# Cross attention on one core: masks as four 64x64 products with shifted heads, and the maxima's score units as two products of 64 rows each

## The chip, the core and the metric

The kernel is one program on one core of a Trainium2 chip. Its engines run beside one another and meet only through semaphores: TensorE (PE in the rows; its weight loads are PEld), VectorE (DVE), ScalarE (ACT), GpSimd (POOL) and SyncE (SP). The metric is the device time of one execution, in microseconds (us), as a median over runs. The change touches the first of two phases, the cross attention.

## The reference

For each of 16 batch rows, 256 tokens of 128 numbers attend to 1600 keys and one more, in 16 heads of 8 dimensions each; a gated residual follows, and then six layers of a second network, which the change leaves alone.

```python
# x (16,256,128), ctx (16,1601,128), mask (16,1,256,1601), NEG = -1e9
def _L0_xattn_ref(q, k, v, mask, ...):
    qh = _split_heads(q @ w_q + b_q)
    kh = _split_heads(k @ w_k + b_k)
    vh = _split_heads(v @ w_v + b_v)
    scores = einsum('bhqd,bhkd->bhqk', qh, kh) / sqrt(8)
    scores = where(mask, NEG, scores)
    attn = softmax(scores, axis=-1)
    out = einsum('bhqk,bhkd->bhqd', attn, vh)
    ...
    return out @ w_o + b_o
x = x + tanh(g_xattn[0]) * _L0_xattn_ref(_layernorm(x), ctx, ctx, mask, ...)
x = x + tanh(g_ffn[0]) * _L0_ffn_ref(_layernorm(x), ...)      # six layers
```

## The kernel before

**Rows, groups and steps.** `cross_phase` works through the 16 batch rows as a pipeline. An `iteration` has a current row `cur`, whose exponentials and products run, a next row `nxt`, which is prepared, and a previous one `prev`, which is finished. It has four parts q = 0 to 3 (four heads each) of KT = 13 steps kt = 0 to 12 (128 keys each, the last 65), 52 steps in all. A step is written (q, kt) here.

**Exact scores in bf16.** Queries and keys are split into three bf16 parts. All nine products of parts are stacked along the contraction, so a head's scores are one product of 9 x 8 = 72 rows; the operands are `q_op` and `k_op`.

**What PE does in a step, in this order.**
1. *Score units* (L736). To find each query's maximum, scores are computed once with queries on the partitions: per four heads 16 units (two tiles of 128 queries, four heads, two halves of the keys), spread over 13 steps by `units_of`. A unit fills one of the two buffers `b_s` with 1024 or 577 columns; DVE adds the mask `mq` and takes the maximum (L509). They run ahead: from step (2, 7) on (TURN = 7) the units are those of `nxt`'s first four heads, and the wait for their operands stands there (`at == 0`).
2. *Transposed scores*, in two halves i = 0, 1 of two heads each and a bank `b_e[i]` of their own: the mask as an identity times `mk`, 512 columns (L750), then two score products of 75 rows and 256 columns (L754; three rows carry minus the maximum). ACT takes the exponential of each half (L436). A mask product waits until ACT has read the same bank in the step before.
3. *Value products* of the step before (L656): four of 9 columns, in four column tiles of the array side by side (an fp32 product is issued as two matmuls).
4. In 20 of the 52 steps one use of the bank `b_p` (`uses`): four for the maxima's transposition, four for keys (L681), four for values (L688), three for the query and its norm, five for the previous row.

**The orders of SP and ACT.** SP's list in an iteration is written out. Keys go to `k_scr` in DRAM and return as `k_op[q]`, one buffer for each q, by three DMAs of 24 rows (L264); queries go to `q_scr` and return as `q_op` by nine DMAs of 8 rows (L319), issued once the last exponential inputs of q = 1 are done. ACT issues three small DMAs with the maxima in each q after step 9 (L480), in its own order, so exponentials stand behind them.

## Time and profile before

| | us |
|---|---|
| median of 3 runs | 5792.77 (5790.32 to 5793.39) |
| the profiled execution | 5784.99 |
| its span in the profile | 5783.2 |
| PE busy in the span | 5490.1 (95%) |
| ACT, DVE, POOL busy | 3995.5, 3631.9, 2653.2 |

The cross attention takes the first 1990 us or so of the span (about 14 of the page's 40 slices). PE is busy in nearly all of it; a busy PE is not PE at its peak, since the ends of pipelined matmuls are modelled. So in the timeline the distance from one start to the next is what a group costs, not its length.

### The profile page before, as it was taken

The page shows a single profiled execution, that of the slowest core. Times are in us where ns is not written, and L with a number is a line of the kernel's source. Part 1 is how long each engine was busy: PE and PEld are TensorE (multiplying, and loading weights), DVE is VectorE, ACT ScalarE, POOL GpSimd, SP SyncE. Part 2 cuts the span into 40 slices and gives each one's busy share as a digit, 9 for nine tenths or more (in the row PEclk, how much of TensorE's full clock was granted, in tenths as well). Part 3 has the DMA queues.
Part 4 walks back from the last instruction along what each step waited for, and adds up shares of the span by engine and source line. Part 5 has one row for each costly group of instructions (what it writes and reads, how often), then busy time and mean ns, then how long its engine had stood idle before and what let it go on. Part 6 is the DMA issues. An engine that isn't in the chain of part 4 may idle for free.

```text
span 5783.2 us, 146589 instructions
## 1 busy us (share of the span) xinstructions
PE 5490.1 (95%) x51848; PEld 3278.6 (57%) x51848; DVE 3631.9 (63%) x8009; ACT 3995.5 (69%) x10790; POOL 2653.2 (46%) x2284
## 2 busy tenths in 40 slices
PE   5999999999999789999999999999999999999997
PEld 2444444444444356666666666666666666666665
DVE  3666776677667456666666666666666666656664
ACT  2555555555555478787887778787888788878885
POOL 2211221112211166656665666666666666665663
PEclk9999999999999899999999999999999999999999
DMA  3232222222332133333333333333333333333332
GB/s 85 61 71 74 57 73 67 74 64 66 74 75 63 54 103 97 100 104 108 97 100 99 108 100 101 94 109 103 102 93 108 104 104 93 97 115 103 93 98 89
DMA packets 144825, 517.35 MB, mean 89 GB/s; under 512 B 29884, under 2 KB 46140, under 8 KB 125676
## 3 DMA queue, kind: packets, MB, share of 16 engines
q1 hardware_dynamic: 142572, 507.58, 31.0%
q8 instruction: 427, 7.00, 0.5%
q14 instruction: 290, 2.38, 0.1%
q10 hardware_dynamic: 1536, 0.40, 0.0%
HBM read 224.98 MB, written 30.68 MB: 44 GB/s over the span
## 4 chain that ended last, share of the span: by engine, by line
PE 44%; ACT 12%; issue 6%; DVE 2%; POOL 1%; DMA 0%; SPq 0%; ACTq 0%; DVEq 0%; POOLq 0%
PE b_qk L1442 9%; PE b_c L1483 6%; PE b_pt L1381 5%; PE b_o L1401 5%; ACT probs L1144 5%; PE b_sc L1369 4%; PE b_nv L1417 3%; PE b_qk L1453 3%; PE b_sc L1360 2%; ACT L1183 2%; ACT L79 2%; PE b_c L1513 2%; PE b_nv L1513 1%; ACT ln_n L1109 1%; PE b_c L1488 1%
## 5 line engine op out<-in xcount | busy, mean ns | idle before, releaser
L436 ACT ACTIVATE eT<-b_e 128x512 f32<-128x512 f32 (+1 forms) x1664 | 903.2, 594 | 871.5 <-PE b_e L754 751.2
L1144 ACT ACTIVATE probs<-b_sc,nb,rq 128x96 f32<-128x96 f32 (+1 forms) x3072 | 1322.5, 449 | 8.7 <-DVE nb L1277 7.5
L509 DVE CUSTOM_DVE_ANT_0 junk<-b_s,mq 128x1024 bf16<-128x1024 f32 (+1 forms) x1024 | 998.9, 990 | 373.3 <-PE b_s L736 359.1
L1068 POOL TENSOR_TENSOR probs<-probs,rsums 128x512 f32<-128x512 f32 (+1 forms) x768 | 717.2, 934 | 666.4 <-DVE rsums L1213 665.9
L1268 DVE TENSOR_REDUCE b_sc<-b_sc 128x4 f32<-128x512 f32 (+1 forms) x768 | 486.1, 633 | 837.6 <-PE b_sc L1369 837.5
L1131 ACT ACTIVATE probsT<-b_pt 128x512 f32<-128x512 f32 x768 | 455.9, 594 | 579.7 <-PE b_pt L1381 579.7
L1442 PE MATMUL b_qk<-xs,weights 128*128 128x256 f32 x3072 | 740.3, 384 | 59.5 <-ACT sq L1158 31.8
L750 PE MATMUL b_e<-mk,identb 128*128 128x512 bf16 (+1 forms) x1664 | 636.7, 383 | 20.6 <-ACT eT L436 19.9
L1144 ACT ACTIVATION_READ_ACCUMULATOR probs<-b_sc,nb,rq 128x1 f32 x3072 | 645.9, 210 | 0.0
L754 PE MATMUL b_e<-q_op,k_op 75*128 75x256 bf16 (+1 forms) x3328 | 639.8, 273 | 0.0
L1442 PEld LDWEIGHTS b_qk<-xs,weights 128*128 128x128 f32 x3072 | 556.4, 191 | 144.9 <-issue 74.5
L1401 PEld LDWEIGHTS b_o<-probsT,v 128*64 128x64 f32 x9216 | 373.0, 137 | 453.3 <-issue 453.3
L1247 DVE TENSOR_TENSOR rot_s<-b_qk,rot_tab 128x512 f32<-128x512 f32 x768 | 525.3, 684 | 127.2 <-PE b_qk L1442 114.7
L1037 POOL TENSOR_TENSOR kT<-kT,rot_p 128x1024 f32<-128x1024 f32 x192 | 454.6, 2368 | 306.1 <-DMA rot_p<-rot_s 302.5
L1401 PE MATMUL b_o<-probsT,v 128*64 128x64 f32 (+1 forms) x9216 | 515.7, 247 | 34.2 <-DVE oT L1205 26.9
L736 PE MATMUL b_s<-k_op,q_op 72*128 72x512 bf16 (+1 forms) x2048 | 504.0, 343 | 27.2 <-DVE smax L509 13.7
L1158 ACT ACTIVATE sq<-b_qk 128x512 f32<-128x512 f32 x768 | 439.1, 599 | 125.1 <-DVE kT L1253 65.5
L656 PE MATMUL b_pv<-eT,vx 128*9 128x256 f32 x6656 | 518.1, 383 | 2.8 <-ACT eT L436 2.8
L1381 PE MATMUL b_pt<-ident,probs 128*128 128x128 f32 x3072 | 504.0, 287 | 1.1 <-POOL probs L1068 1.1
L1045 POOL TENSOR_TENSOR kT<-kT,rkb 128x1024 f32<-128x1024 f32 x192 | 452.1, 2355 | 110.8 <-DMA rkb<-rk_scr 110.8
L1037 POOL TENSOR_TENSOR qT<-qT,rot_p 128x1024 f32<-128x1024 f32 x192 | 453.0, 2359 | 89.5 <-DMA rot_p<-rot_s 70.4
L754 PEld LDWEIGHTS b_e<-q_op,k_op 75*128 75x128 bf16 (+1 forms) x3328 | 332.4, 100 | 252.5 <-issue 5.2
(133 smaller groups left out, 8348.8 us busy)
## 6 DMA issues: line engine op xcount, KB each, us to landing
rot_p<-rot_s SPq DMA_DIRECT2D x768, 256.0 KB, 2.4
rkb<-rk_scr SPq DMA_DIRECT2D x192, 512.0 KB, 6.4
k_op<-k_scr SPq DMA_DIRECT2D x192, 300.2 KB
v<-v SPq DMA_DIRECT2D x192, 256.0 KB, 3.6
k_scr<-kp SPq DMA_DIRECT2D x48, 400.2 KB, 3.5
weights<-in_ffn_w SPq DMA_DIRECT2D x27, 512.0 KB, 5.0
ctxT<-in_ctx SPq DMA_DIRECT2D x17, 800.5 KB, 8.7
q_op<-q_scr SPq DMA_DIRECT2D x144, 64.0 KB
```

The costliest lines, as they stand in the source:

```text
L436: nc.scalar.activation(eT[0:n, g % 2, i * 512:(i + 1) * 512], b_e[i][0:n, :], ACT.Exp).then_inc(s["e_ready"], 1)
L509: nc.vector.tensor_tensor_reduce(junk[:, half, 0:n], b_s[u % 2][:, 0:n], mq[:, p, qt, half * 1024:half * 1024 + n], 1.0, LOWEST, ALU.add, ...
L656: last = nc.tensor.matmul(b_pv[32 * h:32 * h + DK + 1, 0:S], vx[0:n, p, kt, 4 * q + h, :], eT[0:n, g % 2, h * S:(h + 1) * S], start=(kt == ...
L750: nc.tensor.matmul(b_e[i][0:n, :], identb[0:n, 0:n], mk[0:n, p, kt, :].unsqueeze(1).to_broadcast([n, 2, S]), start=True, stop=False, skip_ ...
L754: last = nc.tensor.matmul(b_e[i][0:n, j * S:(j + 1) * S], k_op[q][0:MROW + 3, 2 * i + j, kt * P:kt * P + n], q_op[0:MROW + 3, p, 4 * q + 2 ...
L1037: nc.gpsimd.tensor_tensor(dst, dst, rot_p[:, i % 2, :].rearrange("p (j t) -> p j t", j=4), ALU.add).then_inc(s["sum_ready"], 1)
L1068: nc.gpsimd.tensor_tensor(pu, pu, rsums[:, u % 2, :].unsqueeze(2).to_broadcast([P, 4, w]), ALU.mult).then_inc(s["pn_ready"], 1)
L1144: last = nc.scalar.activation(probs[:, t, k % 2, 2 * e + h, c0:P], b_sc[:, 512 * e + h * w:512 * e + (h + 1) * w], ACT.Exp, bias=nb[:, k % ...
L1247: nc.vector.tensor_tensor(per_block(rot_s[:, q % 2, 512 * (i % 2):512 * (i % 2 + 1)]), per_block(src), rot_tab[:, tab + 1, :].unsqueeze(1) ...
L1381: last = nc.tensor.transpose(b_pt[:, i * P:(i + 1) * P], probs[:, t, u % 2, i, :], ident[:, :])
L1401: last = nc.tensor.matmul(b_o[r, o0 + q0:o0 + q1], v[:, p, tile, vc], probsT[:, u % 2, c + q0:c + q1], start=True, stop=True, skip_group_c ...
L1442: last = nc.tensor.matmul(b_qk[:, 512 * (i % 2) + x * S:512 * (i % 2) + (x + 1) * S], weights[:, c0:c0 + P], xs[:, p, :], start=True, stop ...
```

## The change

- **Masks as quarters (L793 after).** A full mask tile is now four products of 64 rows and 64 columns of the array, 512 columns long: for b_e[0] the two on the diagonal, for b_e[1] the two off it. Off the diagonal, keys come out shifted by 64, so the two heads of i = 1 work on keys kt x 128 + 64 on. `k_op`, `ctxT` and `mk` are longer by 64 keys (wrapped around), and the values of every second pair of heads are computed for shifted keys: each value product of 128 columns becomes two of 64. All four mask quarters stand ahead of both halves' scores.
- **Score units (L770 after).** A unit is two products of 64 rows and 401 columns, one from rows 0 to 63 and one from rows 64 to 127, into two banks. The smallest of the nine products of parts is left out, which gives 64 rows. The operands are new: `k_s`, two buffers with the key's two halves on the two halves of the partitions, and `q_s`, which holds the queries twice. DVE reads 2 x 401 columns for every unit.
- **Loads.** `k_op` has two buffers in place of four. For each q, ten DMAs load `k_s` beside the three for `k_op`; for each row, 16 DMAs of 8 rows load `q_s` beside the nine for `q_op`. SP's list is written anew around these.

PE's order in one step with one unit. Before (the names: b_s the units' banks, b_e the transposed scores, b_pv the values):

```order
L736 MATMUL b_s<-k_op,q_op 128x512 [waits s_max]
L736 MATMUL b_s<-k_op,q_op 128x512
L736 MATMUL b_s<-k_op,q_op 128x512 [waits s_max]
L736 MATMUL b_s<-k_op,q_op 128x65
L750 MATMUL b_e<-mk,identb 128x512 [waits e_ready]
L754 MATMUL b_e<-q_op,k_op 128x256 x2
L750 MATMUL b_e<-mk,identb 128x512 [waits e_ready]
L754 MATMUL b_e<-q_op,k_op 128x256 x2
L656 MATMUL b_pv<-eT,vx 9x256 [waits e_ready]
L656 MATMUL b_pv<-eT,vx 9x256 x3
```

That step has two units. One of the changed kernel, with one unit:

```order
L770 MATMUL b_s<-k_s,q_s 128x401 [waits s_max]
L770 MATMUL b_s<-k_s,q_s 128x401
L793 MATMUL b_e<-mk,identb 64x512 [waits e_ready]
L793 MATMUL b_e<-mk,identb 64x512
L793 MATMUL b_e<-mk,identb 64x512 [waits e_ready]
L793 MATMUL b_e<-mk,identb 64x512
L805 MATMUL b_e<-q_op,k_op 128x256 x4
L688 MATMUL b_pv<-eT,vx 9x256 [waits e_ready]
L688 MATMUL b_pv<-eT,vx 9x256 x3
```

The mask of the second half, with its wait for ACT, now stands ahead of the first half's scores.

SP's list from the start of q = 2 (e_done) to the end of q = 2. Before:

```order
L310 DMA q_scr<-qp 128x256 x2
L319 DMA q_op<-q_scr 8x4096 [waits start_in,e_done,qscr_in]
L319 DMA q_op<-q_scr 8x4096 x8
L264 DMA k_op<-k_scr 24x6404 x3
L264 DMA k_op<-k_scr 24x6404 [waits e_done,start_in]
L264 DMA k_op<-k_scr 24x6404 x2
```

After:

```order
L343 DMA q_scr<-qp 128x256 x2
L280 DMA k_s<-k_scr 16x4x801 [waits e_done,s_done,kscr_in]
L280 DMA k_s<-k_scr 16x4x801 x2
L283 DMA k_s<-k_scr 8x4x801 x2
L280 DMA k_s<-k_scr 16x4x801 x3
L283 DMA k_s<-k_scr 8x4x801 x2
L286 DMA q_s<-q_scr 8x4096 [waits qscr_in]
L286 DMA q_s<-q_scr 8x4096 x15
L272 DMA k_op<-k_scr 24x6660 x3
L263 DMA ctxT<-in_ctx 128x1665 [waits vx_ready]
```

Where nine DMAs of `q_op` stood, ten of `k_s` and 16 of `q_s` stand now; `q_op` moved to the start of q = 3, where `k_s` and `k_op` of the next row stand ahead of it.

```diff
--- before.py
+++ after.py
+TURNED = DH
+KEXT = KEYS + TURNED
+CHUNK = 401
+S_HALF = 800
+S_KEYS = S_HALF + 1
+MASKED = 4 * CHUNK
...
-        k_op = [sb(f"k_op{i}", [P, 4, KEYS], BF16) for i in range(4)]
+        k_op = [sb(f"k_op{i}", [P, 4, KEXT], BF16) for i in range(2)]
+        k_s = [sb(f"k_s{i}", [P, 4, S_KEYS], BF16) for i in range(2)]
+        q_s = sb("q_s", [P, 2, HX, S], BF16)
...
             def load_k(b, p, q):
                 src = k_scr[p].rearrange("c (d h) k -> (c d) h k", d=DK)[:, 4 * q:4 * q + 4, :]
                 for a in range(3):
-                    sp.dma_start(k_op[q][24 * a:24 * a + 24, :, :], src).then_inc(kop_in[q], 16)
-
-
+                    sp.dma_start(k_op[q % 2][24 * a:24 * a + 24, :, :], src).then_inc(kop_in[q % 2], 16)
+
+            def load_ks(b, p, q):
+                src = k_scr[p].rearrange("c (d h) k -> (c d) h k", d=DK)[:, 4 * q:4 * q + 4, :]
+                for tile in range(2):
+                    keys = slice(S_HALF * tile, S_HALF * tile + S_KEYS)
+                    for a in range(3):
+                        r = DH * tile + 16 * a
+                        sp.dma_start(k_s[q % 2][r:r + 16, :, :], src[0:16, :, keys]).then_inc(ks_in[q % 2], 16)
+                    for a in range(2):
+                        r = DH * tile + 48 + 8 * a
+                        sp.dma_start(k_s[q % 2][r:r + DK, :, :], src[16:24, :, keys]).then_inc(ks_in[q % 2], 16)
+
+            def load_q_parts(dst, r, p, a, done):
+                sp.dma_start(dst[r:r + DK, p, :, :], q_scr[p, a].rearrange("(d h) q -> d h q", d=DK)
+                             ).then_inc(s[done], 16)
+
+            def load_qs(p):
+                for tile in range(2):
+                    for a in range(3):
+                        for c in range(2):
+                            load_q_parts(q_s, DH * tile + 16 * a + DK * c, p, a, "qs_in")
+                    for a in range(2):
+                        load_q_parts(q_s, DH * tile + 48 + DK * a, p, a, "qs_in")
...
+            def load_q(p):
+                for a in range(3):
+                    for c in range(3):
+                        load_q_parts(q_op, 24 * a + DK * c, p, a, "qop_in")
...
+                if cur:
+                    sp.wait_ge(s["s_done"], count("s_done", cur[0], 48))
+                    sp.wait_ge(s["e_done"], count("e_done", cur[0], 4 * KT))
                 if nxt:
                     b, p = nxt
-                    sp.wait_ge(start_in, 48)
-                    sp.wait_ge(s["e_done"], count("e_done", b, 6 * KT, back=1))
-                    load_k(b, p, 2)
-                    sp.wait_ge(start_in, 48)
+                    load_ks(b, p, 0)
+                    sp.wait_ge(s["qscr_in"], count("qscr_in", b, 48))
+                    load_qs(p)
+                if cur:
+                    load_k(*cur, 3)
+                if nxt:
+                    b, p = nxt
                     sp.wait_ge(s["vx_ready"], count("vx_ready", b, 4))
                     load_ctx(b + 1)
-                    sp.wait_ge(start_in, 48)
+                    if cur:
+                        sp.wait_ge(s["s_done"], count("s_done", cur[0], 64))
+                        sp.wait_ge(s["e_done"], count("e_done", cur[0], 6 * KT))
+                    load_ks(b, p, 1)
+                    load_k(b, p, 0)
+                    load_q(p)
...
                         nc.vector.tensor_tensor_reduce(
-                            junk[:, half, 0:n], b_s[u % 2][:, 0:n], mq[:, p, qt, half * 1024:half * 1024 + n],
+                            junk[:, half, :].rearrange("p (c n) -> p c n", c=2),
+                            b_s[u % 2][:, :].rearrange("p (c n) -> p c n", c=2)[:, :, 0:CHUNK],
+                            mq[:, p, qt, 2 * CHUNK * half:2 * CHUNK * half + 2 * CHUNK].rearrange("p (c n) -> p c n", c=2),
                             1.0, LOWEST, ALU.add, ALU.max, smax[:, half, 4 * qt + h:4 * qt + h + 1]
...
-                            last = nc.tensor.matmul(b_p[0:n, t * P:(t + 1) * P], ctxT[:, k0:k0 + n],
-                                                    w_sb[:, XW_V:XW_V + P], start=True, stop=True)
+                            wv = w_sb[:, XW_V:XW_V + P].rearrange("p (g i e) -> p g i e", g=4, i=2)
+                            to = b_p[0:n, t * P:(t + 1) * P].rearrange("p (g i e) -> p g i e", g=4, i=2)
+                            for i2 in range(2):
+                                last = nc.tensor.matmul(to[:, :, i2, :], ctxT[:, k0 + TURNED * i2:k0 + TURNED * i2 + n],
+                                                        wv[:, :, i2, :], start=True, stop=True)
...
-                                pe.wait_ge(kop_in[sq], b * KOP + KOP)
-                                pe.wait_ge(s["qop_in"], count("qop_in", b, 9 * 16))
+                                pe.wait_ge(ks_in[sq % 2], (2 * b + sq // 2 + 1) * KS)
+                                pe.wait_ge(s["qs_in"], count("qs_in", b, 16 * 16))
                             for u in units_of(at):
                                 qt, h, half = u // 8, (u // 2) % 4, u % 2
 
                                 pe.wait_ge(s["s_max"], count("s_max", b, 16 * sq + u - 1))
                                 for c in range(2):
-                                    k0 = half * 1024 + c * 512
-                                    n = min(512, KEYS - k0)
-                                    last = nc.tensor.matmul(b_s[u % 2][:, c * 512:c * 512 + n],
-                                                            q_op[0:MROW, p, 4 * sq + h, qt * P:(qt + 1) * P],
-                                                            k_op[sq][0:MROW, h, k0:k0 + n], start=True, stop=True)
+                                    r = slice(c * DH, (c + 1) * DH)
+                                    last = nc.tensor.matmul(b_s[u % 2][:, 512 * c:512 * c + CHUNK],
+                                                            q_s[r, p, 4 * sq + h, qt * P:(qt + 1) * P],
+                                                            k_s[sq % 2][r, h, 400 * half:400 * half + CHUNK],
+                                                            start=True, stop=True)
                                 last.then_inc(s["s_done"], 1)
                         if cur:
                             b, p = cur
                             n = tile_keys(kt)
                             g = q * KT + kt
                             if kt == 0:
+                                pe.wait_ge(kop_in[q % 2], (2 * b + q // 2 + 1) * KOP)
+                                pe.wait_ge(s["qop_in"], count("qop_in", b, 9 * 16))
                                 pe.wait_ge(s["mk_ready"], count("mk_ready", b, 1))
                                 pe.wait_ge(s["mrow_in"], count("mrow_in", b, 48 * (q + 1)))
+                            if n == P:
+
+                                pe.wait_ge(s["e_ready"], count("e_ready", b, 2 * g - 1))
+                                for i in range(2):
+                                    if i:
+                                        pe.wait_ge(s["e_ready"], count("e_ready", b, 2 * g))
+                                    for to in range(2):
+                                        frm = (to + i) % 2
+                                        r, ro = slice(frm * DH, (frm + 1) * DH), slice(to * DH, (to + 1) * DH)
+                                        nc.tensor.matmul(b_e[i][ro, :], identb[r, r],
+                                                         mk[r, p, kt + (i and to), :].unsqueeze(1).to_broadcast([DH, 2, S]),
+                                                         start=True, stop=False, skip_group_check=True)
                             for i in range(2):
 
-                                pe.wait_ge(s["e_ready"], count("e_ready", b, 2 * g + i - 1))
-                                nc.tensor.matmul(b_e[i][0:n, :], identb[0:n, 0:n],
-                                                 mk[0:n, p, kt, :].unsqueeze(1).to_broadcast([n, 2, S]),
-                                                 start=True, stop=False, skip_group_check=True)
+                                if n < P:
+                                    pe.wait_ge(s["e_ready"], count("e_ready", b, 2 * g + i - 1))
+                                    nc.tensor.matmul(b_e[i][0:n, :], identb[0:n, 0:n],
+                                                     mk[0:n, p, kt + i, :].unsqueeze(1).to_broadcast([n, 2, S]),
+                                                     start=True, stop=False, skip_group_check=True)
+                                k0 = kt * P + TURNED * i
                                 for j in range(2):
                                     last = nc.tensor.matmul(
-                                        b_e[i][0:n, j * S:(j + 1) * S], k_op[q][0:MROW + 3, 2 * i + j, kt * P:kt * P + n],
+                                        b_e[i][0:n, j * S:(j + 1) * S], k_op[q % 2][0:MROW + 3, 2 * i + j, k0:k0 + n],
```

## Rows read from the trace of the kernel before

**Rows 1.** Busy time in one stretch (columns in its first line).
```profile
core 0: us, PE busy (x) PEld busy (x) DVE busy (x) ACT busy (x) POOL busy (x), PEclk, DMA share, GB/s
880.00:1000.00 120.00, 118.21 (x939) 53.20 (x938) 83.99 (x165) 64.56 (x119) 23.68 (x26) 1.00 0.29 70
```

**Rows 2.** Timeline, PE and ACT, part of a step: start, length us, what, count.
```profile
1002.37 0.38 PE L754 MATMUL b_e<-q_op,k_op 75*128 75x256 bf16 x2
...
1002.59 0.38 PE L750 MATMUL b_e<-mk,identb 128*128 128x512 bf16 x1
...
1002.79 1.08 ACT L436 ACTIVATE eT<-b_e 128x512 f32<-128x512 f32 x2 [1.14 <-PE b_e L754]
1002.81 0.38 PE L754 MATMUL b_e<-q_op,k_op 75*128 75x256 bf16 x2
...
1003.12 0.62 PE L656 MATMUL b_pv<-eT,vx 128*9 128x256 f32 x8
...
1003.67 0.60 PE L736 MATMUL b_s<-k_op,q_op 72*128 72x512 bf16 x2
```

**Rows 3.** Timeline, PE, the first step of q = 2.
```profile
989.08 0.38 PE L754 MATMUL b_e<-q_op,k_op 75*65 75x256 bf16 x2
...
989.94 0.42 PE L736 MATMUL b_s<-k_op,q_op 72*128 72x512 bf16 x2
```

**Rows 4.** Timeline, SP issuing DMAs, in this row and in the next.
```profile
989.55 2.99 SPq L319 DMA_DIRECT2D q_op<-q_scr  x9
992.58 1.12 SPq L264 DMA_DIRECT2D k_op<-k_scr  x3
...
1107.14 2.99 SPq L319 DMA_DIRECT2D q_op<-q_scr  x9
```

**Rows 5.** Busy time around two batches of loads (columns of Rows 1).
```profile
989.40:990.40 1.00, 1.00 (x12) 0.35 (x12) 0.64 (x2) 0.73 (x2) 0.00 (x0) 1.00 0.00 0
990.40:993.40 3.00, 3.00 (x30) 1.34 (x28) 2.04 (x4) 1.68 (x4) 0.00 (x0) 1.00 0.57 98
990.40:1004.90 14.50, 14.50 (x122) 6.29 (x120) 9.52 (x21) 7.74 (x15) 0.00 (x0) 1.00 0.65 105
977.60:983.60 6.00, 6.00 (x55) 3.01 (x53) 3.64 (x7) 3.26 (x6) 3.22 (x6) 1.00 0.79 178
```

**Rows 6.** Timeline, PE, four 64x64 products in the later phase.
```profile
3002.28 0.30 PE L1360 MATMUL b_sc<-lmask,identb 64*64 64x256 bf16 x4
```

**Rows 7.** DVE instructions by shape: busy us, mean ns | idle before.
```profile
L509 DVE CUSTOM_DVE_ANT_0 junk<-b_s,mq 128x1024 bf16<-128x1024 f32 x512 | 626.1, 1223 | 272.6 <-PE b_s L736 260.9 <-DVE smax L588 8.3 <-issue 3.0
```

**Rows 8.** Timeline, PE, one v unit and what follows.
```profile
1086.46 1.16 PE L688 MATMUL b_p<-w_sb,ctxT 128*128 128x128 f32 x8
1087.45 0.60 PE L736 MATMUL b_s<-k_op,q_op 72*128 72x512 bf16 x2
```

**Rows 9.** Timeline, ACT, steps 9 and 10 of q = 2.
```profile
1008.71 1.09 ACT L436 ACTIVATE eT<-b_e 128x512 f32<-128x512 f32 x2 [0.89 <-PE b_e L754]
1009.68 1.80 ACTq L480 DMA_DIRECT2D q_op<-mp  x3
1011.58 1.09 ACT L436 ACTIVATE eT<-b_e 128x512 f32<-128x512 f32 x2 [1.78 <-PE b_pv L656]
```

**Rows 10.** Timeline, PE, the start of the first row.
```profile
62.20 1.50 PE L736 MATMUL b_s<-k_op,q_op 72*128 72x512 bf16 x4 [12.33 <-issue]
```

**Rows 11.** Timeline, ACT and PE, end of an idle stretch, first row.
```profile
125.53 1.08 ACT L436 ACTIVATE eT<-b_e 128x512 f32<-128x512 f32 x2 [5.73 <-issue]
...
126.18 0.39 PE L750 MATMUL b_e<-mk,identb 128*128 128x512 bf16 x1 [3.42 <-ACT eT L436]
```

**Rows 12.** Timeline, PE, after an idle stretch at the phase's end.
```profile
1984.26 3.66 PE L717 MATMUL b_p<-ru,w_sb 128*128 128x256 f32 x8 [8.81 <-DVE ru L603]
```

**Rows 13.** Granted clock after these two (columns of Rows 1).
```profile
127.40:141.00 13.60, 13.60 (x61) 5.03 (x54) 4.52 (x10) 5.91 (x11) 5.89 (x2) 0.50 0.47 145
1984.30:1987.60 3.30, 3.30 (x8) 2.45 (x8) 0.00 (x0) 0.00 (x0) 0.00 (x0) 0.50 0.00 0
```

More of the change, by code:

```diff
@@ L70 @@
 X_NVEC = 4
-N_SETX = 2
+N_SETX = 1
+N_SETD = 3
 EXP_LN_TABLES = 6
@@ L268, in _ @@
+            def load_q(p):
+                for a in range(3):
+                    for c in range(3):
+                        load_q_parts(q_op, 24 * a + DK * c, p, a, "qop_in")
             load_ctx(0)
             load_masks(0)
-            sp.wait_ge(set_pool, N_SETX)
-            for i in range(4):
-                sp.dma_start(k_op[i][MROW:MROW + 3, :, :], onesr[:, :].unsqueeze(1).to_broadcast([3, 4, KEYS])
-                             ).then_inc(ones_in, 16)
+            sp.wait_ge(set_dve, N_SETD)
@@ L504, in s_units @@
                         qt, h, half = u // 8, (u // 2) % 4, u % 2
-                        n = 1024 if half == 0 else KEYS - 1024
                         dve.wait_ge(s["s_done"], count("s_done", b, 16 * sq + u + 1))
```

99 lines of the change are left out of this document (49 added, 50 removed).

## The prediction

> **What bounds the kernel now.** I read the timeline of PE first, then who waits for whom, then SP's list of DMAs with the stretches around it. In the cross attention PE is busy for 118.2 of 120 us at full clock, DVE for 84, ACT for 64.6, and the DMA engines move 70 GB/s [rows 1]. So PE sets the pace, and what takes work off PE is worth its full length until something else is late. A batch row repeats every 117.6 us: the nine DMAs of `q_op` are issued at 989.55 and again at 1107.14 [rows 4].
>
> In the timeline of a step the reader is to see distances from start to start. Mask to scores 0.22 us, two score products 0.22, the second pair 0.31 up to the value products, and these 0.55 up to the next unit [rows 2]. The second pair takes 0.09 more than the first, though it is the same work: behind it PE goes from full columns to column tiles. Two pairs of scores (0.53), two masks (0.44) and the values (0.55) are 1.52 us. From the first unit of (2, 0) at 989.94 to that of (2, 7) at 1003.67 there are 7 steps in 13.73 us, 1.96 each [rows 2, 3]; so score units cost 0.44 a step.
>
> **What the change takes off PE.** A unit has 800 columns on average before; two products of 401 side by side take half, so 0.44 becomes 0.22. The masks: in the later phase four 64x64 products of 256 columns last 0.30 us together, from the first start to the last end, less than the 0.38 of one full mask of 512 [rows 2, 6]. So quarters do run side by side, and four of 512 columns should cost about one mask, 0.22 in place of 0.44.
>
> Against that stand two more changes of tiling in a step (units to quarters, quarters to full scores), 0.09 each by the step from scores to values: 0.18. PE's own step is then 0.22 + 0.22 + 0.18 + 0.53 + 0.55 = 1.70 us. If such a change cost nothing it would be 1.52, and I know no reason for more than the 0.09 seen.
>
> **What is late next.** All mask quarters now stand ahead of the first half's scores, so these wait until ACT has read both banks of the step before. The loop: first score pair to ACT's start 0.42 (1002.37 to 1002.79), two exponentials 1.08, ACT's end to PE's mask 0.06 (half of the pair's 1.08 after 125.53 is 126.07, the mask starts at 126.18, so 0.11 at most; I take 0.06, since the two overlap a little), masks 0.22, tiling 0.09: 1.87 us [rows 2, 11]. That is more than 1.70. A plain step falls from 1.96 to 1.87 only, and half of the freed time turns into a wait for ACT. In the 20 steps that also use `b_p` PE has more to do (and one more change of tiling, 0.09) and stays the bound: 1.79 in place of 1.96.
>
> DVE reads 802 columns per unit, at 1223 ns for 1024 [rows 7] about 0.96 us where the mean was near that already; its 84 us in 120 cover it. POOL's masks grow by a few per cent and have slack (23.7 of 120 busy [rows 1]). I cost both at nothing.
>
> Per batch row:
> - 25 plain steps outside the stretch (2, 0) to (2, 6): 25 x -0.09 = -2.3 us.
> - 20 steps with `b_p`: 20 x -0.17 = -3.4 us.
> - Values: 26 more matmuls of 64 columns with 128-column loads. A unit of eight now takes 0.99 us to the next start, 0.12 each [rows 8]. If the weight load sets that pace, they cost 26 x 0.12 = +3.1; if the moving columns do, 0. I take 3.1: 128 columns of fp32 have to be loaded as before.
> - The maxima's DMAs: ACT issues three in 1.80 us after step 9, and the next exponentials start 1.78 us after the last ended, where 0.89 is usual [rows 9]. PE does not show that now. In a loop that hangs on ACT it does: 1.78 - (1.87 - 1.08) = 1.0 us. Twice in full (q = 2, 3), twice half covered by `b_p` work in step 9 (q = 0, 1): 3.0, less 0.6 that I allow for what is lost already: +2.4. Bounds 0 and 4.
>
> **The stall.** The first unit of the next row, at (2, 7), needs `q_s` and `k_s`. SP may start them only when q = 1's scores are done, and in the trace it issues 0.47 us after the last pair (989.08 to 989.55); no byte moves before 990.4, 0.85 us on [rows 3 to 5]. Before, nine `q_op` DMAs (9 x 64 = 576 KB) had to be there by 1003.67. Now it is ten of `k_s` (128 rows of 4 x 801 bf16, 820 KB) and then 16 of `q_s` (1024 KB), on one queue.
> - `q_op` alone moved at 98 GB/s, with `k_op` behind it at 105; `k_op` alone in 977.6 to 983.6 (some small writes beside it) at 178 [rows 5]. `q_s` has exactly the shape of `q_op` (8 rows of 8 KB): 1024 KB / 98 = 10.4 us. `k_s`, short pieces of 1.6 KB, lies between 178 and 98: 4.6 to 8.4 us. I take the mixed 105, 7.8 us.
> - Landed at 990.4 + 18.2 = 1008.6, where the unit started at 1003.67: +4.9 us. Bounds: 15.0 us of transfer give +1.7, 18.8 give +5.5.
> PE takes its instructions in order, so behind this wait stand all scores and values; ACT and DVE drain, and nothing covers it. The seven steps before it become faster, but that only lengthens the wait.
>
> The DMA engines' busy share was 0.57 while `q_op` ran alone, against 0.79 for `k_op` [rows 5]: DMAs of 8 rows leave many engines idle. The Trainium skill, "DMA: Bandwidth & Descriptors", section "Why a DMA increments its semaphore by 16 and not by 1", says that a DMA runs on the largest number of engines up to 16 that divides its outer sizes, the lowest-numbered ones; so 8 rows go to the same 8 engines each time, and the trace agrees. If that did not hold and `q_s` ran at 178 GB/s, all would have landed at 1000.8, ahead of need.
>
> **Clock.** After 3.42 us without PE work the granted clock was 0.50 (1.2 in place of 2.4 GHz) for the 13.6 us of 127.4 to 141.0, with PE busy in all of it; after an idle 8.81 us it was still 0.50 for 3.3 us of work [rows 11 to 13]. At half clock half the work is lost: 6.8 and 1.7 us. The stall is between these in length; I take 3.0 a row, bounds 0 and 6.8.
>
> **Sum.** -2.3 - 3.4 + 3.1 + 2.4 + 4.9 + 3.0 = +7.7 us a row, in 15 iterations that have a next row: +115. The very first units start after 12.33 us without PE work, at 62.20 [rows 10]; they now wait for `k_s` (7.8 us) and seven more DMAs of 64 KB (4.6), +12; the last row, with no stall and fewer units, gives back about 6. Together +121 us on the profiled execution's 5785, so 5906. The median of the runs shown is 7.8 us above that execution: 5914 us, 2.1% slower.
>
> **The rivals.**
> 1. *The loads arrive in time.* For it: the batch 977.6 to 983.6 ran at 178 GB/s. Against: DMAs of just this shape did not. At that rate landing is 1000.8, no stall, no lost clock; in the stretch (2, 0) to (2, 6) the steps gain 7 x 0.09 = 0.6. -2.3 - 3.4 - 0.6 + 3.1 + 2.4 = -0.8 a row, -12: 5781. With values and ACT's DMAs free as well, -6.3 a row: 5698. Other side of the forecast; it decides from 18.2 us of transfer down to about 12.5. Chance 0.24.
> 2. *The quarters, or a unit's two products, do not overlap.* Both quarters of a bank come from different rows of the array at once. In the later phase the rows write different banks, so the trace does not show this case. If they take turns, the masks cost 0.44 again, PE's step is 1.91: 25 plain steps lose 0.04 each and 20 others 0.22, +5.4 a row, +81: 5995. The Trainium skill, "TensorEngine Tiling (Array Packing)", "Restrictions and Gotchas", says that different row tiles cannot use the same PSUM bank simultaneously; by it this rival would be the case. Here the two write different partitions of the bank, which is why I give it less. Chance 0.14.
> 3. *The stall is there, but short and at full clock,* and values follow the moving columns: -2.3 - 3.4 + 0 + 2.4 + 1.7 = -1.6 a row, with +6 for the start: 5775. Chance 0.06.
> The forecast itself has 0.56; with its costs at their far ends (clock 6.8, stall 5.5) it reaches 5980. Its own range is 5850 to 5980.
>
> A difference under 0.2% (12 us) can't be told from none. Of rival 1, about half lies within that (5781 is at its edge), half is faster; rival 3 is faster; the forecast's low edge gives a little to "same". Faster 0.20, same 0.10, slower 0.70. The range for 8 in 10: 5755 to 5995.
>
> **What would show it.** In the profile after: at each (2, 7) PE idle for about 5 us ahead of the unit, released by the `q_s` DMAs, with the clock at 0.50 behind it; plain steps of 1.87 us with waits of the masks for ACT; the four quarters within about 0.4 us of each other's ends; 0.09 us at each change of tiling; 16 value matmuls at 0.11 to 0.12 us. The forecast is wrong if `q_s` lands before step (2, 7), if the clock holds through the stall, or if PE's steps come near 1.70 us.

## The result, and the profile after

The changed kernel takes 6128.8 us (median of 4 runs, 6102.7 to 6200.5) against 5792.4 us before: a ratio of 1.0566, 95% interval 1.0519 to 1.0613, 336 us more. The forecast was 5914 us with a range up to 5995. The execution that was profiled is the slowest of the four, 6200.5 us, more than 1.5% above the fastest, so the ratio leaves it out; e6 and e7 below show what is said of the clock in runs near their medians. Against the 5785 us of the profiled one before it takes 415 us more, and the sums below are made against these; 72 us of them lie above the median.

I read the stall first. PE at step (2, 7) of one row (columns as in [rows 2]):

```profile
start us, us, engine line op out<-in xcount [idle before <-releaser]
1042.89 0.62 PE L688 MATMUL b_pv<-eT,vx 128*9 128x256 f32 x8
1054.27 0.52 PE L770 MATMUL b_s<-k_s,q_s 64*128 64x401 bf16 x2 [10.75 <-DMA q_s<-q_scr]
1054.71 0.64 PE L793 MATMUL b_e<-mk,identb 64*64 64x512 bf16 x4
```

It is where the forecast put it and is released by `q_s`, but lasts 10.75 us and not 4.9. The length of a step is counted here from its first exponential to that of the next step, so a wait ahead of one step lengthens the one before: this stall shows in step (2, 6). Over rows 1 to 14 that step takes 12.18 us on average where it took 1.97 before: 10.2 us more. SP's issues ahead of it:

```profile
1029.93 1.27 SPq L280 DMA_DIRECT2D k_s<-k_scr  x3
...
1033.95 5.38 SPq L286 DMA_DIRECT2D q_s<-q_scr  x16
1039.37 1.12 SPq L272 DMA_DIRECT2D k_op<-k_scr  x3
1040.54 0.36 SPq L263 DMA_DIRECT2D ctxT<-in_ctx  x1
```

In the list of packets `k_s` moves from 1030.9 to 1037.7 and `q_s` from 1037.2 to 1052.9. The stretches (the seventh number is the granted clock, then DMA share and GB/s):

```profile
core 0: us, PE busy (x) PEld busy (x) DVE busy (x) ACT busy (x) POOL busy (x), PEclk, DMA share, GB/s
1030.80:1037.10 6.30, 6.30 (x64) 2.46 (x60) 5.03 (x10) 3.28 (x7) 0.00 (x0) 1.00 0.78 128
1037.10:1053.00 15.90, 6.41 (x66) 2.27 (x64) 4.39 (x11) 4.32 (x8) 0.00 (x0) 0.84 0.86 117
1054.30:1081.90 27.60, 27.60 (x166) 7.67 (x166) 11.68 (x24) 9.56 (x18) 2.48 (x5) 0.50 0.35 72
1082.10:1105.60 23.50, 20.41 (x198) 7.50 (x194) 13.84 (x29) 10.95 (x21) 2.50 (x5) 1.00 0.82 127
```

The third row is the larger surprise: behind the stall PE is busy for 27.6 us without a gap, and the clock stays at 0.50 (1.2 GHz) all that time. [Rows 13] showed 13.6 us at most. Two more waits were on no list of mine: ahead of the masks of (0, 0), here of the next row, and of (0, 11), which is inside the step counted as (0, 10):

```profile
1105.67 0.48 PE L793 MATMUL b_e<-mk,identb 64*64 64x512 bf16 x4 [2.61 <-DMA q_op<-mp]
...
991.42 0.89 PE L793 MATMUL b_e<-mk,identb 64*64 64x512 bf16 x4 [1.41 <-ACT eT L466]
```

The first waits for the three small DMAs of the maxima, which ACT issued 10 us earlier, at 1095.61. The second was there before, a little shorter and with the clock full behind it, as PE's timeline of the kernel before has it:

```profile
1073.33 0.39 PE L750 MATMUL b_e<-mk,identb 128*128 128x512 bf16 x1 [0.97 <-ACT eT L436]
```

Now the clock falls behind it too. A steady step of the changed kernel, PE's timeline, and ACT's in a like step:

```profile
1084.22 0.60 PE L793 MATMUL b_e<-mk,identb 64*64 64x512 bf16 x4
1084.76 0.61 PE L805 MATMUL b_e<-q_op,k_op 75*128 75x256 bf16 x4
1085.30 0.62 PE L688 MATMUL b_pv<-eT,vx 128*9 128x256 f32 x8
1085.85 0.34 PE L770 MATMUL b_s<-k_s,q_s 64*128 64x401 bf16 x2
1086.12 0.60 PE L793 MATMUL b_e<-mk,identb 64*64 64x512 bf16 x4
...
1094.82 1.08 ACT L466 ACTIVATE eT<-b_e 128x512 f32<-128x512 f32 x2 [0.82 <-PE b_e L805]
```

1.90 us from mask to mask, of which ACT works 1.08 and waits 0.82 for the scores: the loop of the forecast. Where nothing waits, quarters to scores take 0.34 us (1082.51 to 1082.85); here 0.54, the rest being a wait for ACT.

The account of a row, from the first exponentials of one row to those of the next (mean of rows 1 to 14): 117.7 us before, 144.7 after, +27.0. The steps' medians at full clock, stall left out, add up to 119.2, which is +1.6; the stall is +10.2; what is left, **+15.2, is the half clock** and the waits at (0, 0). Fourteen times 27.0 is 379 us; row 0 adds 13, the start 8, the last row 7 and the phase behind it 8, together the 415. PE was busy at half clock for 574 us of the cross attention, before for 17 us.

### The profile page after: what moved, and what is told of

Read it like the earlier page. It is cut to its first block, busy times and chain, and to the rows that moved or that the text cites. A ratio compares the mean times of both kernels' runs of the same rounds, so it can differ in the third digit from the quotient of the medians.

```text
span 6198.7 us, 151308 instructions
## 1 busy us (share of the span) xinstructions
PE 5710.0 (92%) x53800; PEld 3254.5 (53%) x53800; DVE 3640.5 (59%) x8011; ACT 4004.0 (65%) x10790; POOL 2661.7 (43%) x2283
## 4 chain that ended last, share of the span: by engine, by line
PE 41%; ACT 12%; issue 5%; DVE 2%; POOL 1%; DMA 0%; SPq 0%; ACTq 0%; DVEq 0%; POOLq 0%
PE b_qk L1493 9%; PE b_c L1534 6%; PE b_pt L1432 5%; PE b_o L1452 5%; ACT probs L1195 4%; PE b_sc L1420 3%; PE b_nv L1468 3%; PE b_qk L1504 3%; PE b_sc L1411 2%; ACT L1234 2%; ACT L86 2%; PE b_c L1564 2%; PE b_nv L1564 1%; ACT ln_n L1160 1%; PE b_c L1539 1%
## 5 line engine op out<-in xcount | busy, mean ns | idle before, releaser
L540 DVE CUSTOM_DVE_ANT_0 junk<-b_s,mq 128x802 bf16<-128x802 f32 x1024 | 998.4, 991 | 571.1 <-PE b_s L770 558.0
L805 PE MATMUL b_e<-q_op,k_op 75*128 75x256 bf16 (+1 forms) x3328 | 588.0, 302 | 0.0
L688 PE MATMUL b_pv<-eT,vx 128*9 128x256 f32 x6656 | 578.9, 424 | 2.8 <-ACT eT L466 2.7
L770 PE MATMUL b_s<-k_s,q_s 64*128 64x401 bf16 x2048 | 355.2, 375 | 173.5 <-DMA q_s<-q_scr 147.4
L387 POOL CAST mp<-mneg 4x256 bf16<-4x256 f32 x64 | 27.7, 432 | 1106.0 <-DVE mneg L555 1106.0
L793 PE MATMUL b_e<-mk,identb 64*64 64x512 bf16 x3072 | 421.0, 442 | 65.9 <-DMA q_op<-mp 30.7
```

The costliest lines, as they stand in the source:

```text
L540: nc.vector.tensor_tensor_reduce(junk[:, half, :].rearrange("p (c n) -> p c n", c=2), b_s[u % 2][:, :].rearrange("p (c n) -> p c n", c=2)[ ...
L688: last = nc.tensor.matmul(b_pv[32 * h:32 * h + DK + 1, 0:S], vx[0:n, p, kt, 4 * q + h, :], eT[0:n, g % 2, h * S:(h + 1) * S], start=(kt == ...
L805: last = nc.tensor.matmul(b_e[i][0:n, j * S:(j + 1) * S], k_op[q % 2][0:MROW + 3, 2 * i + j, k0:k0 + n], q_op[0:MROW + 3, p, 4 * q + 2 * i ...
```

## The experiments

"Half clock" is the time in the cross attention in which PE was busy at the granted clock 0.50, summed from the trace; the changed kernel has 574 us (676 with its idle time, the figure that some expectations name). A "gap" is an idle time of PE. Each ratio is to runs of the kernel before that were taken beside the run.

| run | kernel | us (median) | ratio, 95% interval | half clock, us |
|---|---|---|---|---|
| e1 | changed, loads early | 5966.2 | 1.030 (1.024-1.036) | 291 |
| e2 | e1 with whole masks | 5821.9 | 1.006 (1.004-1.007) | 65 |
| e3 | before, with quarters | 6008.2 | 1.034 (1.028-1.040) | 347 |
| e4 | before, with a stall | 6078.4 | 1.050 (1.049-1.052) | 104 |
| e5 | changed, whole masks | 5987.7 | 1.034 (1.032-1.035) | 158 |
| e6 | changed, values undoubled and unshifted | 6063.5 | 1.044 (1.039-1.049) | 413 |
| e7 | changed, q_s by 16 rows, read twice | 6255.8 | 1.078 (1.072-1.084) | 449 |
| e8 | e2, such loads, spread | 5953.2 | 1.027 (1.026-1.029) | 106 |
| e9 | e5, values doubled, masks ahead of scores | 6037.0 | 1.043 (1.041-1.044) | 165 |
| e10 | changed, copies of q | 6054.3 | 1.046 (1.045-1.048) | 369 |
| e11 | e2, copies, spread | 5878.9 | 1.015 (1.014-1.017) | 121 |
| e12 | e2, spread | 5845.0 | 1.009 (1.008-1.011) | 104 |
| e13 | e1, copies, gated, list reordered | 5874.8 | 1.014 (1.011-1.017) | 188 |
| e14 | e2, copies, gated, list reordered | 5742.6 | 0.992 (0.991-0.994) | 9 |
| e15 | e2, gated, list reordered | 5765.7 | 0.996 (0.994-0.997) | 45 |

**e1: the loads early.** Only the place of one wait differs:

```diff
                     sp.wait_ge(s["s_done"], count("s_done", cur[0], 48))
-                    sp.wait_ge(s["e_done"], count("e_done", cur[0], 4 * KT))
 ...
                 if cur:
+                    sp.wait_ge(s["e_done"], count("e_done", cur[0], 4 * KT))
                     load_k(*cur, 3)
```

> The changed kernel with one difference: SP no longer waits for q = 1's scores (e_done 4 KT) ahead of k_s and q_s of the next row, but only ahead of k_op for q = 3, which now follows them. The loads can start at step (1, 6) in place of (2, 0), 25 us ahead of the units that need them, for 18 to 21 us of data. Theory 1 (the loss is the loads' stall at (2, 7), about 10 us a row, and the half clock that it and the smaller waits bring): no gap of PE at (2, 7), steps at full clock as they were (their medians in the changed kernel add up to 119.2 us a row, stall left out), so 5785 + 15 x 1.6 + 10 for the start = about 5820 us (5780 to 5870), half-clock time in the cross attention under 150 us. Rival A (the sparser steady state of quarters and half units drops the clock by itself): the stall goes, 10 us a row, but the clock still falls for 300 us or more: 5950 to 6050 us. Rival B (the stall is not the price, the steps are): about 6100 us.

Measured 5966 us, with 291 us of half clock. The stall at (2, 7) is gone from every row (step (2, 6) 1.90 us), but this gave back 163 us and no more. So theory 1 alone is out; the time is rival A's, but the run does not show that the stream loses the clock by itself, as small waits are left. New ones stand at (2, 0), 2 to 5 us in nine of 14 rows, and at (0, 0), 1 to 3.3 us, for the maxima's DMAs:

```profile
1134.71 0.59 PE L793 MATMUL b_e<-mk,identb 64*64 64x512 bf16 x4 [3.20 <-DMA q_op<-mp]
```

**e2 and e3: one half of the change each.** In e2 the masks and values are as before:

```diff
-                                        nc.tensor.matmul(b_e[i][ro, :], identb[r, r], ...   # four quarters
+                                nc.tensor.matmul(b_e[i][0:n, :], identb[0:n, 0:n],
+                                                 mk[0:n, p, kt, :].unsqueeze(1).to_broadcast([n, 2, S]), ...
```

> Only the score units of the change (two products of 64 rows from k_s and q_s), masks as one 128x128 product each and values undoubled as in the kernel before; loads early as in e1_early. PE's step by the terms of the forecast: 1.96 - 0.22 + 0.09 = 1.83 us, above ACT's loop since each mask waits for its own bank alone. Theory 1: no stall, full clock, 52 steps a row at -0.13 in the 40 that PE bounds = -5 us a row, 15 rows: 5792 - 78 + 10 for the start = 5725 us (5690 to 5770). Rival A (row tiles of 64 rows by themselves cost clock): half clock in more than a tenth of the cross attention, 5850 us or more. Rival B: the change of tiling eats the gain, 5785 to 5810 us.

Measured 5822: outside all three ranges, between rivals B and A, with little half clock, but a wait of up to 5.5 us ahead of the masks of (0, 0), the step (3, 12), released by `q_op<-mp` (48 us of idle in all). e3 has the quarters, the shifted heads and the doubled values in the kernel before, with its own units and loads:

> Only the masks of the change (64x64 quarters with shifted heads, doubled value products), score units and all loads as in the kernel before. Nothing is loaded in addition, so no stall at (2, 7). Theory 1: full clock; plain steps 1.90 to 1.92 us in place of 1.96, three value steps at +0.7 each: between -0.5 and +1.5 us a row, 5785 to 5815 us. Rival A (a PE that waits a little for ACT in each step loses the clock): half clock for 100 us or more in the cross attention, 5880 us or more.

Measured 6008: rival A in size (5880 or more), but not in form. Ten rows run at full clock, 122.6 us each: +5.0 on the row before. Two rows take 195 and 190 us (below one row at full clock, then a part of the second slow one):

```profile
1640.00:1760.00 120.00, 118.13 (x1020) 49.31 (x1016) 81.12 (x159) 62.51 (x114) 22.88 (x24) 1.00 0.28 69
1800.80:1960.00 159.20, 159.19 (x826) 53.11 (x827) 57.49 (x121) 48.37 (x90) 17.95 (x20) 0.50 0.19 47
```

In the second stretch PE is never idle, and the clock does not return for 160 us. It had fallen behind a gap of 1.3 us. So quarters and doubled values by themselves cost 5 us a row at full clock, and a half clock that has begun can last longer than a row with PE busy all the time.

**e4: a stall in the dense kernel.** 22 DMAs of `q_op`'s shape to a place that nobody reads:

```diff
+                    for c in range(SPARE):            # 22
+                        r = DK * (c % 16)
+                        sp.dma_start(spare[r:r + DK, c // 16, :, :], q_scr[p, 0].rearrange(...)).then_inc(spare_in, 16)
                     for a in range(3):                # q_op
```

> The kernel before, with 22 DMAs of 8 rows (64 KB each, read by nobody) issued ahead of the nine of q_op in each row. At q_op's measured 98 GB/s they take 14.7 us, so q_op lands at about 1011 where the unit started at 1003.7: a stall of 7.3 us at (2, 7) in PE's otherwise full stream. Theory 1: the stall also halves the clock for about 10 to 20 us a row behind it; 15 x (7.3 + 5 to 10) + 15 for the start = +200 to +275: 5990 to 6070 us. Rival A (the clock is lost only by the sparser stream of the changed kernel): the stall alone, 15 x 7.3 + 15 = +125, 5917 us, half clock under 3 us a row. If the extra DMAs run faster than q_op's did, there is no stall and 5792.

The gaps are twice what I worked out, 15.3 us in the median:

```profile
1162.12 1.01 PE L745 MATMUL b_s<-k_op,q_op 72*128 72x512 bf16 x2 [16.73 <-DMA q_op<-q_scr]
```

but behind them the half clock lasts only 4.8 us (3.7 to 6.7), where the changed kernel has 13.1 (3.4 to 28.0) behind gaps of 10.3. The total of 6078, 8 us above theory 1's range, is mostly gap (15 x 15.3 = 230 of 288 us). It comes near theory 1's number for the wrong reason, and rival A's 5917 is out too.

**e5, e6, e9: the same stall in front of other streams.** Whole masks (e5), undoubled values (e6, which leaves out the values' shift and so computes other values), whole masks with doubled values (e9), each in the changed kernel with its late loads.

> The changed kernel with its loads as late as they were, but each mask one 128x128 product again and the values undoubled: the same stall of about 10 us at each (2, 7), in front of another stream. Theory 1 (a stall costs its half clock whatever follows): half clock of about 45 us a row as in the changed kernel (676 us in all), 5950 to 6030 us. Theory 2, new after e3 and e4 (the stall or small wait only starts the half clock; how long it lasts depends on what PE then runs, and the 64x64 quarters keep it): half clock of 5 to 10 us a row behind each stall as in e4, under 200 us in all: 5822 of e2 + 15 x (10 + 3) = 5960 to 6020 us with under 200 us of half clock. The half-clock time and its length per event decide, not the total.

> The changed kernel with 13 value products of 128 columns as before, in place of 26 of 64: this leaves out the shift of the values by 64 keys for every second head. It takes away the term of +3.1 us a row (measured +2.1 by the steps (1, 3), (1, 5), (1, 9)). If that is all: 15 x -2 = -30 us on 6129, about 6095 us, and half clock as long as before. If the small weight-bound products are what prolongs the half clock rather than the mask quarters: half clock less than half of 676 us and 5950 us or less.

> The changed kernel, stall, doubled values and order kept, with each step's four mask quarters replaced by two products of 128x128 (both still ahead of the scores); the shift by 64 keys is left out of the second mask. If the quarters are what keeps the half clock: behind each stall of 10 us about 5 us of busy half clock as in e5 (13 in the changed kernel), none after waits of 1 to 1.5 us, half clock under 300 us in all, 5990 to 6050 us. If it is the doubled values or the longer wait for ACT: half clock above 450 us, 6080 to 6150 us.

| | gap at (2, 7), median | half clock behind it, median (range) |
|---|---|---|
| changed | 10.3 us | 13.1 us (3.4-28.0) |
| e6, quarters | 7.9 | 13.1 (3.4-15.2) |
| e7, quarters (below) | 16.8 | 11.7 (4.5-26.8) |
| e5, whole masks | 10.3 | 4.9 (3.5-6.5) |
| e9, whole masks | 10.5 | 5.0 (3.4-6.5) |

One stretch of e5 and one of e9, right behind a gap of 11.23 and of 10.5 us:

```profile
1107.53 0.52 PE L767 MATMUL b_s<-k_s,q_s 64*128 64x401 bf16 x2 [11.23 <-issue]
...
1107.60:1111.00 3.40, 3.40 (x18) 0.98 (x17) 1.00 (x2) 1.19 (x2) 0.00 (x0) 0.50 0.57 123
1111.20:1150.00 38.80, 34.75 (x309) 13.34 (x308) 24.52 (x51) 19.52 (x36) 4.96 (x10) 0.98 0.69 115
```

```profile
999.70:1003.30 3.60, 3.60 (x18) 0.96 (x17) 1.00 (x2) 1.09 (x2) 0.00 (x0) 0.50 0.60 130
1003.60:1030.00 26.40, 25.94 (x232) 10.31 (x230) 18.04 (x38) 14.62 (x28) 3.36 (x7) 1.00 0.62 112
```

e9 differs from the changed kernel in the quarters alone (the second mask's shift, which it leaves out, changes values and not work), and the long half clock is gone: theory 2 holds. e6 keeps the quarters and keeps most of it, 413 us. Its 65 us of gain are more than the 30 expected, but its gap is shorter by 2.4 us in the mean too, and with the 2.1 us of the value steps that is 15 x 4.5 = 67 us. Whether the doubled values also add to the half clock is not settled.

**e7 and e8: q_s by DMAs of 16 rows.**

```diff
-                        for c in range(2):
-                            load_q_parts(q_s, DH * tile + 16 * a + DK * c, p, a, "qs_in")
+                        sp.dma_start(q_s[r:r + 16, p, :, :], q_scr[p, a].rearrange("(d h) q -> d h q", d=DK)
+                                     .unsqueeze(0).to_broadcast([2, DK, HX, S])).then_inc(s["qs_in"], 16)
```

> The changed kernel with q_s loaded by 8 DMAs of 16 rows in place of 16 of 8 rows: the same bytes, source rows read twice by one DMA, nothing moved. The forecast took 10.4 us for q_s because DMAs of 8 rows use half of the engines. If that was right, q_s lands in 5 to 6 us less, the gap at (2, 7) falls from about 10 to about 5 us, but the half clock behind it mostly stays: 15 x -5 = -75 us, 6020 to 6080 us. If the number of rows is not what limits q_s (Rival), the gap stays 9 to 11 us and the time 6100 to 6160 us.

> e2 with the loads spread: q_s by 8 DMAs of 16 rows and q_op by 3 of 24 rows, q_op ahead of the next k_s, so that the maxima's small DMAs no longer stand behind a backlog at (3, 9). In e2 the last step lasts 4.6 us where it lasted 2.58, and (0, 1) runs at half clock in 11 of 14 rows. Theory: that wait goes (2.0 us a row) and the 72 us of half clock with it (2.4 a row): 5822 - 15 x 4.4 = 5756 us (5735 to 5785), faster than the kernel before. Rival (the small DMAs are late for another reason): 5810 to 5825 us.

Both missed (6020 to 6080 and 5735 to 5785 were expected), by my own making. e7's gap grew to 16.8 us in the median, 17.20 in this row, and `q_s` took 23 us, at a DMA share of 0.49:

```profile
1077.00:1100.00 23.00, 6.38 (x66) 2.27 (x64) 4.35 (x11) 4.28 (x8) 0.00 (x0) 0.70 0.49 110
```

Six of the eight DMAs have an outer size of 2 (the repetition), not 16. The Trainium skill's rule, "DMA: Bandwidth & Descriptors", "Why a DMA increments its semaphore by 16 and not by 1", gives them two engines; the trace agrees, since 96 packets of about 0.47 us at two engines are 22.6 us, and at the end of `q_s` packets of 0.31 us come eight in 1.24 us, two at a time. e8 carried the same loads. Its rows still showed that the wait at (3, 12) goes with the spread order (2.60 us in place of 4.6).

**e10 to e12: 16 different rows.** Each part of q is now written three times to DRAM, and rows are read once:

```diff
+                    for x in range(9):
+                        sp.dma_start(q_scr[p, x], qp[:, x // 3, :]).then_inc(s["qscr_in"], 16)
 ...
+                    for i, x in enumerate((0, 3, 6, 2)):
+                        r = DH * tile + 16 * i
+                        sp.dma_start(q_s[r:r + 16, p, :, :], q_scr[p, x:x + 2].rearrange("c (d h) q -> (c d) h q", d=DK)
```

> The changed kernel with each part of q stored three times in DRAM, so that q_s comes by 8 DMAs of 16 different rows (128 KB each) and q_op by 3 of 24; e7's DMAs had an outer size of 2 and took 23 us for the same bytes. If a DMA runs on as many engines as its outer size allows: q_s in 6 to 8 us in place of 15.7, the gap at (2, 7) falls from 10 to 0 to 3 us, time near e1's 5966 us (5930 to 6010). If not: gap 8 us or more and 6080 us or more.

> e2 (whole masks, half units) with the loads spread (q_op ahead of the next k_s) and the copies of e10. e8 showed that the wait at (3, 12) goes with the spread (2.60 us in place of 4.6), but its slow q_s brought the stall back. Here both should be away: 5822 - 15 x 2.0 for (3, 12) - 5 for (2, 6) - half of 65 us of busy half clock = 5755 us (5735 to 5780), faster than the kernel before. Rival: more small waits move in elsewhere, 5790 to 5830 us.

> e11 without the copies: q_s in 16 DMAs of 8 rows, q_op in 9. Same bytes as e2, in the spread order. If the order is what matters: within 15 us of e11. If the DMAs of 8 rows keep the queue full for too long: waits of 1 to 3 us at (2, 0) or (2, 7), half clock behind them, 5790 to 5840 us.

e10's gap fell to 4 us (step (2, 6) 6.10 us in place of 12.18), a little more than the 0 to 3 expected, and the half clock mostly stayed, so its 6054 us lie above the range. e11's 5879 us lie outside both of its ranges. In e11 only one wait was left, at (3, 0), in every row:

```profile
1050.45 1.80 ACTq L511 DMA_DIRECT2D q_op<-mp  x3
...
1061.66 0.58 PE L785 MATMUL b_e<-mk,identb 128*128 128x512 bf16 x1 [4.91 <-DMA q_op<-mp]
```

The three DMAs of 2 KB each take 10 us from issue to landing: `k_op`, the context and `q_op` are ahead of them (in the updates of the semaphores `q_op` ends at 1059.1). In the kernel before the last packet of such a group ended 0.7 or 0.8 us behind its third issue all 64 times; in e11 it ended 6.1 to 8.9 us behind it once in each row that has a next one. The same wait had been at (2, 0) in e1, at (3, 12) in e2. It is one wait that moves with the backlog. e12 was 34 us faster than e11, outside its expected range by 5 us, and slower than e2: the spread order alone gains nothing.

**e13 to e15: SP holds the bulk back until the small DMAs have landed.**

```diff
+                        sp.wait_ge(s["mrow_in"], count("mrow_in", cur[0], 4 * 48))
                     load_ks(b, p, 1)
                     load_q(p)
 ...
                     load_k(b, p, 0)
+                    sp.wait_ge(s["mrow_in"], count("mrow_in", b, 48))
                     load_ctx(b + 1)
```

The order of the list changed with it: against e11, `k_s` goes ahead of `q_op` again and the context comes last, so the gain is that of both together.

> The changed kernel's quarters, doubled values and half units, with early loads, the copies of q, and SP holding the next bulk loads (k_s, q_op, k_op, then the context and the masks) until the maxima's small DMAs of q = 3 and of the next q = 0 have landed. No wait for a DMA should be left. If quarters lose the clock only behind waits: full clock in over 95% of the cross attention, rows of 117 to 118 us, 5785 to 5815 us. If they lose it by themselves (or behind the 1.3 us wait of PE at (0, 10), which no load causes): half clock of 150 us or more, 5860 to 5950 us.

> e11 with the same gating: in e11 the small DMAs issued at step (2, 9) landed 10 us later, behind k_op, the context and q_op, and PE waited 5 us at (3, 0). The medians of e11's steps at full clock, with that wait taken out, add up to 113.0 us a row against 117.6 in the kernel before: 15 x -4.6 + 8 for the start = 5730 us (5715 to 5760), 1% faster than the kernel before. If a wait only moves again (to (3, 7) for k_s or to (0, 3) for the context): 5770 to 5840 us.

> e14 without the copies of q: q_s in 16 DMAs of 8 rows. q_s takes 15.7 us in place of about 10, so it should land near step (2, 5), still ahead of (2, 7): within 10 us of e14 if nothing else is late; 5770 to 5800 us with short waits at (2, 0) or (2, 7).

e14 takes 5742.6 us and is faster than the kernel before by 0.8% (interval 0.64 to 0.91%). All of its rows from 1 to 14 last 114.9 to 115.2 us at full clock:

```profile
1043.03 0.39 PE L787 MATMUL b_e<-mk,identb 128*128 128x512 bf16 x1 [1.15 <-ACT eT L469]
...
1013.00:1127.90 114.90, 112.43 (x922) 45.88 (x921) 83.16 (x164) 63.66 (x117) 24.10 (x26) 1.00 0.58 114
```

My 113.0 for its row left out one step, (3, 1), that never ran at full clock in e11; with its 2.0 us the sum is 115. e13, with quarters and two waits for a DMA (2.1 and 1.1 us, at (2, 0)), has rows of 118.6 us at full clock, but at the wait of (0, 10), which no load causes, it loses the clock in 8 rows of 14:

```profile
981.75 0.98 PE L796 MATMUL b_e<-mk,identb 64*64 64x512 bf16 x4 [1.41 <-ACT eT L469]
...
982.40:1023.40 41.00, 41.00 (x218) 16.76 (x216) 14.81 (x33) 14.15 (x27) 7.34 (x4) 0.50 0.52 115
1334.40:1453.00 118.60, 115.35 (x1044) 47.53 (x1042) 83.13 (x164) 63.74 (x117) 24.12 (x26) 1.00 0.57 111
```

Its 5875 us lie in the range of the second case. e15, with waits of 1.1 to 2.7 us ahead of (2, 7) in nine rows, takes 5766 us, between its two forecasts, and shows what the copies are worth: 23 us.

## Why the prediction was wrong

- **The mechanism was right.** Late `q_s` stalls PE at (2, 7), and the stall and the clock behind it decide the sign. Rival 1 (the loads arrive in time) and rival 3 did not happen.
- **Rival 2 is refuted.** A unit's two products start 3 ns apart, as do two quarters that write one bank. The rule of the Trainium skill that I named with it ("TensorEngine Tiling (Array Packing)", "Restrictions and Gotchas"), that different row tiles cannot use the same PSUM bank simultaneously, is not borne out here: the measurement decides.
- **The terms of a plain step were right.** PE's own step, waits left out, is 0.27 + 0.34 + 0.54 + 0.55 = 1.70 us, the 1.70 of the forecast, and ACT's loop holds it at 1.90 (forecast 1.87). Values: 16 matmuls of 64 columns in 1.93 us at full clock (below), 0.12 each. The three value steps of a row grew by 2.1 us, steps' savings included (forecast +3.1 alone).

```profile
1022.58 2.00 PE L723 MATMUL b_p<-w_sb,ctxT 128*128 128x64 f32 x16
1024.51 0.34 PE L770 MATMUL b_s<-k_s,q_s 64*128 64x401 bf16 x2
```

- **ACT's DMAs** (+2.4) cost nearly nothing: steps (2, 9) to (2, 11) take 6.2 us in e13 and took 6.2 before. But the plain steps' gain was too large: it was taken against a mean of 1.96, while steps whose unit has 577 columns took 1.78 before and take 1.90 now. At full clock a row came to +1.6 us, where the forecast's terms without stall and clock are -0.2; 1.0 of the 1.6 is a wait at (0, 0), since step (3, 12) takes 3.74 us here and 2.73 in e13.
- **The step that failed first is the stall's transfer time.** `k_s` took 6.8 us (7.8 forecast), `q_s` 15.7 and not 10.4. The 98 GB/s [rows 5] are the rate of the first 3.0 us of `q_op`, when packets start closer together, and I carried it over to all of `q_s`. The same trace's list of packets has the nine DMAs from 990.4 to 998.6: 576 KB in 8.15 us, 72 GB/s. e4 shows that this is the rate with nothing beside it; eight packets of 8 KB start every 0.91 us there (columns of [rows 1]):

```profile
1136.75:1142.20 5.45, 5.45 (x49) 2.29 (x48) 3.39 (x8) 3.19 (x6) 0.00 (x0) 1.00 0.52 72
```

  At 72 GB/s `q_s` takes 14.5 us, lands at 1012.7 and stalls PE for 9.0 us, beyond my upper bound of 5.5. The last 1.2 of the 15.7 us come with slower packets (1.1 to 1.4 us each between 1046.6 and 1051.3), while `k_op` and the context, issued from 1039.4 on, move too; that these slow them was not tried. 10.2 for 4.9: +5.3 a row.
- **The step that failed most is the clock's.** I took 3.0 a row with 6.8 as the bound, from two recoveries in front of the old stream [rows 13]. It was 15.2, together with the waits at (0, 0); with all of the 72 us above the median taken off it, 4.8 a row, 10.4 would be left. e4 shows that the bound was fair for the old stream (4.8 us of half clock), and e5 and e9 against the changed kernel that quarters make the same gap cost more than twice the recovery. Nothing in the trace of before had a long run of quarters behind a gap, and I should have kept that end open rather than bound it by the nearest rows.
- **Not on the list at all** were the small DMAs of the maxima. The change loads 4.3 MB a row more (four times 820 KB of `k_s` and 1 MB of `q_s`). The same 100 us of the timeline (busy time in stretches), of the changed kernel and of the one before:

```profile
1000.00:1100.00 100.00, 88.88 (x756) 34.26 (x752) 51.94 (x110) 42.15 (x80) 11.99 (x18) 0.83 0.59 104
```

```profile
1000.00:1100.00 100.00, 98.50 (x776) 44.12 (x775) 71.18 (x139) 54.25 (x100) 20.35 (x25) 1.00 0.24 66
```

The DMA share is more than twice what it was. I looked for a bulk transfer that comes late, and not for a small one that stands behind it.

What stays open: why the clock stays low under quarters. That PE is busy in every nanosecond there is shown; what differs between 64x64 quarters and a whole product, for the chip, is not. Quarters are not the only way to a long recovery either: in the first row, whose stream is another, whole masks have 13.6 us of it in the kernel before [rows 13] and 15 us in e4, e5 and e15.

## What to carry to other kernels

An idle time on PE of more than 2 us cost its length and then a recovery at half clock in 211 of 213 cases here (rows 1 to 14 of all runs, clock full before the gap), and the price depends on the stream that follows: measure it in front of the new stream, not the old. Before adding bulk loads, list the small DMAs that an engine waits for, and let the queue hold the bulk back until they have landed; here that, with the new order of the list, was worth 79 us (e12 to e15), and 136 where the copies were in (e11 to e14). And before a rate is read from a stretch, look at whether the stretch holds the whole transfer. Packing products side by side pays only where PE is what the step waits for, and each change of tiling takes back about 0.1 us: from a unit of 401 columns to the quarters it is 0.27 us, where 0.17 would do at the 0.22 us that 512 columns of a full mask take [rows 2] (an estimate).

## What the runs showed of the hardware

- PE at half clock with no idle time stayed there for 160 us and more (e3), 54.6 us (e10), and 41 us (the changed kernel three times, e7 twice, e13 once), all with quarters in the stream; with whole masks the longest such time was 15.4 us (e5, in the first row).
- Gaps and the clock, in rows 1 to 14, for gaps that begin at full clock. With whole masks, gaps of 1.0 to 1.5 us, most of them 1.15, left it at full in all of 120 cases (the kernel before, e2, e4, e5, e8, e11, e12, e14, e15); in e9, whose gaps are most of them 1.25, 3 of 15 lost it. With quarters, gaps of 1.0 to 1.5 us, most of them 1.4, lost it in 68 of 94 (the changed kernel, e1, e6, e7, e10, e13), gaps of 1.25 in 2 of 14 (e3). At about 1.25 us whole masks (e9, at (0, 10)) and quarters (e3) lost it equally often, 2 times in 14, so the length of the gap may be the whole difference here, and the streams can't be compared by this.
- The rate of DMAs of 8 rows, 8 KB a row, one behind another: 98 GB/s in the first 3 us (the kernel before), 72 GB/s from then on (e4).
- A load of 1 MB took 23 us with six of its eight DMAs repeating their source through an outer size of 2 (e7), 15.7 us as 16 DMAs of 8 rows, and 10.4 us as DMAs of 16 different rows (e11, from its first landing, 1031.6, to its last, 1042.0).
- Two 64x64 products from different rows of the array that write different partitions of one bank start 3 ns apart (the changed kernel, 1084.220 and 1084.223).
